# A graph layer with three places reordered: the fold of the query weights, the slice loop's divide, and the attention's inverse

## The reference

```
xn = layernorm(x)
x  = x + gnn(xn, edges) + mix(xn)
     gnn: filt = silu(attr @ Wf1 + bf1) @ Wf2 + bf2;  msg = xn[col] * filt
          agg = segment_sum(msg, row);  h = silu(agg @ Wu1 + bu1) @ Wu2 + bu2;  xn + batchnorm(h)
     mix: k = softmax(k, over nodes);  context = k^T v (8 heads of 32);  (q context) * gate @ Wproj + bproj
y  = layernorm(x)
     fx = y @ W_fx + b_fx;  w = softmax((y @ W_x + b_x) @ W_slice ..., over 64 slices, 8 heads)
     token = sum_n(fx * w) / (sum_n(w) + 1e-5)
     q, k, v = token @ W_q, token @ W_k, token @ W_v;  out = softmax(q k^T / 8) v
x  = x + (w out) @ W_out + b_out
```

## Time and profile before

| what | value |
|---|---|
| median of 3 runs | 2125.78 us (2119.08 to 2127.16) |
| profiled execution | 2126.19 us, span 2124.4 us |
| busy share PE / PEld / DVE / ACT / POOL | 89 / 72 / 71 / 63 / 68% |
| edge loop, first hidden product to last scatter | 151.2 to 1662 us |
| slice loop, first logits to last token product | 1820.2 to 2016.3 us |
| attention, to the first output product | 2016.6 to 2044.5 us |
| output products | 2044.5 to 2118 us |
| VectorE steps of the fold, L1350 / L1356 (two) / L1361 | 0.69 / 0.61 / 0.69 us |
| SP's queue in chunk 2: last window load before, next issue after | up to 191.8, from 197.05 us |
| VectorE steps L2158 / L2160 / L2165 / L2167 | 0.68 / 0.67 / 0.62 / 0.68 us |

### The profile page before, as it was taken

The page is one execution under the profiler, slowest core; times in us unless marked ns, Lnnn a source line. Parts: engine busy times, 40 slices in busy tenths (PEclk is TensorE's granted clock), DMA queues, the critical chain, the costliest instruction groups (busy, mean ns, idle before and its releaser), DMA issues. The chain is left out here.

```text
span 2124.4 us, 38305 instructions
## 1 busy us (share of the span) xinstructions
PE 1887.8 (89%) x9824; PEld 1537.4 (72%) x9824; DVE 1509.5 (71%) x3450; ACT 1347.4 (63%) x2410; POOL 1454.9 (68%) x997
## 2 busy tenths in 40 slices
PE   4988999899899989998899989998996397799998
PEld 3666888787777777777687767786775376577678
DVE  6966877777676767767677677676674297788746
ACT  4546766776676667666676676667664167577723
POOL 2216888888888888888888888888888574355500
PEclk9999999999999999999999999999998599899979
DMA  9777888987888789888888888888887892000002
GB/s 373 312 289 164 159 157 162 174 158 141 168 167 155 139 163 172 153 141 163 169 158 148 165 170 152 144 165 166 150 146 109 228 323 80 12 0 0 1 29 102
DMA packets 288979, 325.41 MB, mean 153 GB/s; under 512 B 30118, under 2 KB 251721, under 8 KB 288688
## 3 DMA queue, kind: packets, MB, share of 16 engines
q0 software_dynamic: 112896, 102.81, 39.2%
q1 hardware_dynamic: 172576, 217.21, 31.7%
q10 hardware_dynamic: 3280, 2.83, 0.5%
HBM read 167.64 MB, written 154.97 MB: 152 GB/s over the span
## 5 line engine op out<-in xcount | busy, mean ns | idle before, releaser
L993 POOL DMA_INDIRECT sums<-x_rows,out_idx x784 | 1238.1, 1579 | 291.4 <-issue 210.9
L1047 PE MATMUL bank<-wf,x_rows 128*128 128x256 f32 x3136 | 797.3, 382 | 0.0
L1047 PEld LDWEIGHTS bank<-wf,x_rows 128*128 128x128 f32 x3136 | 543.4, 191 | 53.5
L1157 ACT ACTIVATE x_rows<-bank,bf 128x512 f32<-128x512 f32 x392 | 270.3, 689 | 268.4 <-PE bank L1025 264.2
L1252 DVE TENSOR_TENSOR msg_low<-x_rows,msg_high 128x512 fp32r<-128x512 f32 x392 | 272.1, 694 | 170.8 <-ACT msg_high L1177 170.8
L1283 DVE TENSOR_TENSOR x_rows<-bank,x_rows 128x512 f32<-128x512 f32 x392 | 269.0, 686 | 105.1 <-PE bank L1047 99.8
L1177 ACT ACTIVATE msg_high<-x_rows 128x512 fp32r<-128x512 f32 x392 | 247.3, 631 | 93.0 <-DVE x_rows L1283 89.8
L1045 PE MATMUL bank<-gnn_bf_halves,ones 128*128 128x256 f32 x784 | 296.1, 378 | 0.0
L1165 ACT ACTIVATE x_rows<-pair 128x516 f32<-128x516 f32 x392 | 230.5, 588 | 78.5 <-DMA sums<-x_rows,out_idx 77.9
L1184 ACT ACTIVATE x_rows<-bank 128x512 f32<-128x512 f32 x392 | 231.9, 592 | 34.2 <-PE bank L1035 33.8
L1035 PE MATMUL bank<-window,spread 128*128 128x256 f32 x784 | 193.8, 329 | 60.9 <-DVE spread L1247 40.0
(11 more groups left out here) (330 smaller groups left out, 2729.4 us busy)
## 6 DMA issues: line engine op xcount, KB each, us to landing
window<-xn_halves SPq DMA_DIRECT2D x392, 128.0 KB, 4.1
sums<-gate SPq DMA_DIRECT2D x32, 800.0 KB, 10.4
x_rows<-id_rows SPq DMA_DIRECT2D x98, 256.0 KB, 5.2
x_rows<-attr_rows SPq DMA_DIRECT2D x98, 256.0 KB, 4.7
xn_halves<-xn_halves SPq DMA_DIRECT2D x7, 1792.0 KB, 6.6
x_rows<-id_rows SPq DMA_DIRECT2D x98, 128.0 KB, 3.7
sums<-x_rows,out_idx POOLq DMA_INDIRECT x784
res<-sums SPq DMA_DIRECT2D x24, 512.0 KB, 7.7
```

Source lines behind the costliest of these rows:

```text
L993: nc.gpsimd.indirect_dma_start(g.sums_dram[k], bass.IndirectOffsetOnAxis(ap=out_idx[:, ET * c + t:ET * c + t + 1], axis=0), summed[c % 2][ ...
L1047: mm = T.matmul(out, hidT[:, j // 2, f, ds((2 * (j % 2) + t) * P, P)], g.wf2[:, f, :], start=False, stop=f == CB - 1)
L1157: A.activation(hidT[:, h, f, :], hps[:], ACT.Silu, bias=g.bf1[:, f:f + 1]).then_inc(hid_ready, 1)
```

## The change

1. *Fold.* The three TensorE steps of the fold move to places 0, 2 and 4 of the loop's first group, and VectorE's answers to places 1, 3 and 5. Ahead of the loop TensorE only makes the hidden products and the first gather, now behind the first of them. The 13 weight loads move from place 2 to place 9.
2. *Slice loop.* VectorE divides tile t-1 before it shifts tile t. ScalarE's `round_both` is cut in two: `round_w(t-1)` ahead of the exponential, `round_x(t)` at the end of the step; copy of turned weights behind the exponential. POOL: `low_w(t-1)`, then `low_x(t)`. TensorE: turn_x(t+1) ahead of turn_w(t-2). The column sums of W_fx and W_q W_k^T are made in step 1, in the banks of the token sums, and read in step 2 before the token sums begin.
3. *Attention.* The sum of weights is taken as columns: eight products with the sums as stationary operand and one moving column give 128x4 numbers; VectorE scales and inverts these, writes two diagonal blocks, ScalarE two more, and four products of `mean_of` with the diagonals spread the inverse over 64 rows. The token is then (W_fx sums - eps bias) inverse + bias, in three wide VectorE steps. The bias products move to the block's start, and PSUM banks change names.

```diff
-AT_WEIGHTS = 2
+AT_WEIGHTS = 9
+AT_FOLD = (0, 2, 4)
...
+            def context():
+                pe.wait_ge(fold_stage, 1)
+                ...
+            def fold_query():
+                pe.wait_ge(fold_stage, 1 + CB)
...
             def output(s, place):
+                if is_first(s) and place == AT_FOLD[0]:
+                    turn_gram()
+                if is_first(s) and place == AT_FOLD[1]:
+                    context()
+                if is_first(s) and place == AT_FOLD[2]:
+                    fold_query()
...
             hidden(0, 0, 0, 0)
-            pe.wait_ge(fold_stage, 1)
...
+            gather(0, 0)
             hidden(0, 0, 0, 1)
-            pe.wait_ge(fold_stage, 1 + CB)
...
             hidden(0, 0, 1, 0)
-            gather(0, 0)
             along(pe, chunk, output)
...
             high_attr(0, 0)
-            for h, f in ((0, 0), (0, 1), (1, 0)):
-                silu(0, h, f)
+            silu(0, 0, 0)
             copy_rows(0, 0)
+            silu(0, 0, 1)
+            silu(0, 1, 0)
...
+            def weight_products():
+                pe.wait_ge(g.late_in, 16 * len(g.late_weights))
+                pe.wait_ge(small, ONES)
+                for h in range(FH):
+                    for b in range(CB):
+                        nc.tensor.matmul(acc[0][0:FD, ds(h, 1)], g.w_fx[:, b, ds(h * FD, FD)], g.mean_of[:, 0:1],
+                                         start=b == 0, stop=b == CB - 1)
+                nc.tensor.matmul(acc[1][0:FD, 0:FD], g.w_qT, g.w_kT, start=True, stop=True).then_inc(summed_w, 1)
...
             def step(t, r):
                 logits(t, r)
+                if exists(t + 1):
+                    turn_x(t + 1, (r + 1) % RING)
                 if not is_before(t, LAG):
                     turn_w(t - LAG, (r - LAG) % RING)
-                if exists(t + 1):
-                    turn_x(t + 1, (r + 1) % RING)
+                if is_known(t, 1):
+                    weight_products()
+                if is_known(t, LAG):
+                    pe.wait_ge(small, SHIFT_COPIED)
...
             def step(t, r):
+                if is_known(t, LAG):
+                    act.wait_ge(summed_w, 1)
+                    A.activation(g.mix, acc[1][0:FD, 0:FD], ACT.Copy).then_inc(small, 1)
+                if exists(t + 1):
+                    copy_xT(t + 1, (r + 1) % RING)
+                if not is_before(t, 1):
+                    round_w(t - 1, (r - 1) % RING)
+                expo(t, r)
                 if not is_before(t, LAG):
                     copy_w(t - LAG)
...
+                round_x(t, r)
...
             def step(t, r):
+                if is_known(t, LAG):
+                    weight_shift()
+                if not is_before(t, 1):
+                    divide(t - 1, (r - 1) % RING)
                 shift(t, r)
                 if exists(t + 1):
                     low_xT(t + 1, (r + 1) % RING)
-                if not is_before(t, 1):
-                    divide(t - 1, (r - 1) % RING)
...
+            dve.wait_ge(mat, COLS)
+            V.tensor_scalar(inv[:], g.ps[1][:, 0:HGB], EPS, 1.0 / C, ALU.add, ALU.mult).then_inc(vec, 1)
+            dve.wait_ge(vec, SCALED)
+            V.reciprocal(inv[:], inv[:]).then_inc(vec, 1)
+            dve.wait_ge(vec, INVERSE)
+            for q in range(2):
+                op = V.tensor_scalar(diag[:, ds(q * P, P)], g.ident[:], inv[:, q:q + 1], None, ALU.mult)
+            op.then_inc(vec, 1)
             dve.wait_ge(mat, FX)
-            dve.wait_ge(vec, SHARE)
-            V.tensor_tensor(raw, g.ps[3][0:FD, :], raw, ALU.add).then_inc(vec, 1)
+            V.tensor_tensor(heads(raw), heads(g.ps[3][0:FD, :]), wide(g.fx_less[:]), ALU.add).then_inc(vec, 1)
+            dve.wait_ge(mat, SPREAD)
             dve.wait_ge(vec, SUMMED)
-            V.tensor_tensor(fxT[:], raw, inv, ALU.mult).then_inc(vec, 1)
+            V.tensor_tensor(raw, g.ps[0][0:FD, :], raw, ALU.mult).then_inc(vec, 1)
+            dve.wait_ge(vec, DIVIDED)
+            V.tensor_tensor(heads(fxT[:]), heads(raw), wide(g.fx_bias[:]), ALU.add).then_inc(vec, 1)
...
+            for q in range(HGB):
+                for b in range(CB):
+                    mm = T.matmul(g.ps[1][:, ds(q, 1)], tokT[:, b, ds(q * P, P)], mean_of[:, 0:1], start=b == 0,
+                                  stop=b == CB - 1)
...
+            for q in range(HGB):
+                mm = T.matmul(g.ps[0][0:FD, ds(q * P, P)], mean_of[:], diag[:, ds(q * P, P)], start=True, stop=True)
```

More of the change, by code:

```diff
@@ L1303, in chunk, with turned_gram, scaled_context, folded_query @@
                     work(j)
-            def output(s, place):
+            def turned_gram():
+                dve.wait_ge(fold_made, 1)
+                V.tensor_copy(gram.rearrange("p b n -> p (b n)"), bankT[:]).then_inc(fold_stage, 1)
+            def scaled_context():
+                dve.wait_ge(cols_ready, 3)
+                dve.wait_ge(fold_made, 2)
+                for f in range(CB):
+                    V.scalar_tensor_tensor(out=ctx_m[:, f, :], in0=bankK[:, ds(f * P, P)], scalar=k_inv[:, f:f + 1],
+                                           in1=g.head_mask[:], op0=ALU.mult, op1=ALU.mult).then_inc(fold_stage, 1)
+            def folded_query():
+                dve.wait_ge(fold_made, 3)
+                V.tensor_copy(g.wqm[:], bankT[:].rearrange("p (b n) -> p b n", b=CB)).then_inc(fold_stage, 1)
+            def output(s, place):
+                if is_first(s) and place - 1 == AT_FOLD[0]:
+                    turned_gram()
+                if is_first(s) and place - 1 == AT_FOLD[1]:
+                    scaled_context()
+                if is_first(s) and place - 1 == AT_FOLD[2]:
+                    folded_query()
                 if place - 1 in AT_HIDDEN:
@@ L1863, in slice_tokens @@
     acc = token_sums(g)
+    summed_w, small = sem("h_summed_w"), sem("h_small")
+    ONES, SHIFT_COPIED = 1, 3
     heads = lambda ap: ap.rearrange("p (h n) -> p h n", h=FH)
@@ L2051, in step, with weight_shift @@
                     low_xT(t + 1, (r + 1) % RING)
-                if not is_before(t, 1):
-                    divide(t - 1, (r - 1) % RING)
+            def weight_shift():
+                dve.wait_ge(summed_w, 1)
+                V.scalar_tensor_tensor(out=g.fx_bias[:], in0=acc[0][0:FD, 0:FH], scalar=-float(C), in1=g.b_fxT[:],
+                                       op0=ALU.mult, op1=ALU.add).then_inc(small, 1)
+                dve.wait_ge(small, SHIFT_COPIED)
+                V.tensor_scalar(g.fx_less[:], g.fx_bias[:], -EPS, None, ALU.mult)
+            V.memset(g.mean_of[:], 1.0 / C).then_inc(small, 1)
             low_xT(0, 0)
@@ L2205, in _ @@
             A.activation(tokT[:, 0, :], acc[0], ACT.Copy).then_inc(act_done, 1)
-            act.wait_ge(mat, MIX)
-            A.activation(mix, g.ps[7][0:FD, 0:FD], ACT.Copy).then_inc(act_done, 1)
+            act.wait_ge(vec, INVERSE)
+            for q in range(2, HGB):
+                op = A.activation(diag[:, ds(q * P, P)], g.ident[:], ACT.Copy, scale=inv[:, q:q + 1])
+            op.then_inc(act_done, 1)
             high(0)
@@ L2245, in _ @@
             mm.then_inc(mat, 1)
+            pe.wait_ge(vec, DIAG)
+            pe.wait_ge(act_done, DIAG_COPIED)
+            for q in range(HGB):
+                mm = T.matmul(g.ps[0][0:FD, ds(q * P, P)], mean_of[:], diag[:, ds(q * P, P)], start=True, stop=True)
+            mm.then_inc(mat, 1)
             pe.wait_ge(vec, FX_DONE)
-            pe.wait_ge(act_done, MIXED)
-            T.matmul(g.ps[5][0:FD, :], mix, fxT[:], start=True, stop=True).then_inc(mat, 1)
+            T.matmul(g.ps[2][0:FD, :], g.mix, fxT[:], start=True, stop=True).then_inc(mat, 1)
             T.matmul(g.ps[1][0:FD, :], g.w_v, fxT[:], start=True, stop=True).then_inc(mat, 1)
@@ L2261, in _ @@
                 mm.then_inc(mat, 1)
[L2262 to L2264 removed]
             pe.wait_ge(vec, WEIGHED)
             for k in range(HALF_HEADS):
[L2267 removed]
+                mm = T.transpose(g.ps[5][0:FG, ds(k * P, P)], at[:, ds(k * FG, FG)], g.ident[:])
             mm.then_inc(mat, 1)
```

125 lines of the change are left out of this document (50 added, 75 removed).

## The result

The changed kernel takes 2103.36 us (median of 8 runs, 2094.23 to 2110.39); the kernel before takes 2123.34 us in the runs beside it (8 runs, 2118.78 to 2127.16). The ratio is 0.9903, 95% interval 0.9886 to 0.992: 0.97% less, 20 us. The prediction had 2110.5 us with a range of 2101 to 2119. The profiled execution of the changed kernel took 2107.18 us, its span is 2105.4.

What follows compares the result with a forecast made beforehand. The prediction took starved POOL at the edge loop's start, a three-engine circle of waits in the slice loop and the attention's chain as bounds; gains 5.0 + 6.3 + 4.2 = 15.5 from 2126.2 gave 2110.7, stated as 2110.5 us, range 2101 to 2119.

Steps and rivals of the forecast that it cites:

- rival (a): Attention: TensorE's clock stays up, gaining 9 to 10 us more, for 2101 us; chance 0.18.
- First scatter 2.4 us earlier: Edge loop's start: first filter product 3.8 us earlier, less 0.5 for transposes and 0.9 for half clock.
- What feeds POOL, 6.2 ahead less 1.2, gain 5.0: Edge loop's start: POOL's supply 6.2 us ahead by the 21st scatter, less 1.2 for TensorE's waits on VectorE.
- The ids' transfer: Edge loop's start: chunk 2's edge ids no longer behind weight loads; 4.4 us idle and 1.5 slow stretch saved.
- the fold's work in the loop: Edge loop's start: two big fold steps cost 2.1 us, waits for VectorE's added steps 1.2.
- Rival (b): Edge loop's start gains nothing, since loads at place 9 starve VectorE once, 4.6 us; 2115.7 us, chance 0.12.
- Slice loop, 3.66 a tile: Slice loop: tile falls from 3.83 to 3.66 us, limits being 3.53, 3.54 and 3.63; whole gain 6.3 us.
- The small products in step 1: Slice loop's step 1: 17 small products take up to 4 us at half clock, partly hidden; cost 1.6 us.
- (c): Slice loop: the tile stays at 3.75 to 3.83 us as another close limit takes over; 2117 us, chance 0.12.
- (d): Slice loop: ScalarE's exponential is late, 4.36 us a tile, 24.5 us lost; 2141 us, chance 0.06.
- Last tile, 0.5: Slice loop's end: the divide of tile 47 is out of the way before the last shift, gaining 0.5 us.
- Attention, 3.2 to `fxT` and 1.0 for the bias products: Attention: `fxT` complete 3.2 us earlier, bias products leaving their place gain 1.0; together 4.2 us.

Runs made afterwards that it cites:

- e5: The changed kernel itself, run again with a second profile; 2098.91 us, ratio 0.9881 to the kernel before.
- e11: The kernel before with only the weights' loads moved to place 9; 2117.8 us, ratio 0.9965.
- e7: The changed kernel with token-sum products 64 columns wide and two unused 512-column products where TensorE waits; 2098.21 us, ratio 0.9892 to the kernel before.
- e2: The kernel before with the slice loop's new orders on all four engines, without the early sums; 2117.04 us, ratio 0.9965.
- e4: The kernel before with VectorE's new order alone (divide of tile t-1 before shift of tile t); 2116.49 us, ratio 0.9965.
- e12: The kernel before with the fold's move, the loads' place and VectorE's order, nothing else; 2113.36 us, ratio 0.9944.
- e1: The kernel before with the edge loop's part alone (fold moved, weight loads at place 9); 2114.23 us, ratio 0.9962.

## Why the prediction was right, and which steps were not

The total lay within the range, and the places were right, but the gain came out at 20 us where the sum had 15.5. By stretches, and with the mean of the changed kernel's three profiles, the largest part of the difference is 3.4 us from the last logits to the end (109.6, where the sum had 113.0), mainly the full clock of e5; the slice loop has 1.2 more than the sum, the start 0.9. The median lies below the forecast's own 2105 to 2115 us, and the whole range holds it because rival (a) had widened it down to 2101. By its own steps, with the means of the like profiles:

- **First scatter 2.4 us earlier**: 2.5 on the mean, but 1.8 against profiles with as long a half clock as the one that I computed from, and 3.0 with a longer one. The fold's two large products were 1.05 us each at full clock, as said.
- **What feeds POOL, 6.2 ahead less 1.2, gain 5.0**: 5.9. But its terms were off in both directions. The ids' transfer was put at 5.9 (4.4 idle and 1.5 of slow stretch) and is worth 4.6; the fold's work in the loop was put at 3.3 (2.1 + 1.2) and costs 1.2. The prediction named the transfer as the largest piece and then spoke of the fold; e11 says that one constant would have done three quarters of it. (Between the ids' turn and their issue stood eleven loads, all that the program issues at that place, not the 13 that I wrote; their 6.6 us on SP, 165.81 to 172.45, are right.) Rival (b), loads at place 9 starving VectorE, did not happen.
- **Slice loop, 3.66 a tile**: 3.63, my bound of the circle, without the reserve I had added for TensorE's own 3.53 and the transposes' 3.54. Limits that close to each other cost nothing here: 45 x 0.03 is 1.4 us. The small products in step 1 took 2.32 us at a clock that rose midway in the first profile; in e7 they ran at half clock for 3.57:

```profile
1820.99 3.57 PE L1971 MATMUL pair<-mean_of,wide_weights 128*64 128x1 f32 x32
1824.49 0.47 PE L1973 MATMUL pair<-wide_weights 64*64 64x64 f32 x2
```

  Over the kernels with and without them, tiles 0 to 3 take 14.9 and 13.6 us on the mean: 1.3, of my 1.6, though the kernels of either group lie further apart than that (12.4 to 14.5 and 12.8 to 17.4). Rivals (c) and (d) did not happen (the 24.5 us of (d) should read 24.3); the exponential starts 0.03 us after the shift's end (1991.46 + 0.70 to 1992.19).
- **Last tile, 0.5**: 0.5 to 0.6, from the last logits to the attention's first product (10.15 to 9.56, 9.63 with VectorE's order alone). The whole stretch hides it: with the new loop order and the old attention it takes 118.1 on the mean of three, with both old 117.4, so what follows the last tile lost 1.3.
- **Attention, 3.2 to `fxT` and 1.0 for the bias products**: here a step failed as I put it. At the full clock the way to `fxT` is as laid out: 6.98 us from the bias products to the product from `fxT` in e5, 10.01 from the first product to the same place before, so 3.0. What failed is the silent assumption that this stretch keeps its full clock as it did before. It does in some runs (e5) and not in others (0.2 gained in the first profile), and where it does not, TensorE happens to have the full clock back for Q, V and the logits, which gave 2.4 behind `fxT`; the output products gave 1.6, where the half clock lasted 4.4 us into them and not 6.7. The term came out at 4.2 with other contents. The one-column products were put at 1.5, at most 1.7, and took 1.92 at full clock (e5).
- **Rival (a), 9 to 10 us more if the clock stays up**: 8.0 more (104.6 and 112.6), in two of five profiles. I gave it 0.18 as something that either is or is not; it should have been a share of the runs, and the range's lower end should have been lower than 2101: nine of 18 runs lie below it, the lowest at 2093.9. Its argument, less idle time, fits only in part. All six profiles with 3.0 to 4.0 us of idle ahead of `fxT` had fallen before W_out and both with 0.44 had not, but the idle time of 1.49 us is the same in e5, which stayed up, and in the first profile, which did not. What I had set against the rival, that narrow products never brought the clock up again, does not hold: in the first profile it came back at 2010.9, behind the products with W_fx and the spread. The Trainium skill, "TensorE: Matmul & The Clock Gate", section "What's actually happening", says of the other change, the first rise of the clock at a kernel's start, that it is "run-variable" for one and the same kernel. Here the falls are so too: the first one stands 11.6, 26.8 and 13.1 us behind the last logits in three profiles of this kernel.

## What to carry to other kernels

When an engine's queue holds something needed at once behind something needed much later, move that first, and alone: eleven loads at another place brought 4.6 us, the rebuilt fold 1.3. When an engine order is changed in a circle of waits, try each engine by itself: one engine's order brought 7.4 of 8.6 us, and the wait that looked like the cause stayed and cost next to nothing. Cost a chain of narrow products at both clocks, and say in how many runs each may hold; a product into an unused bank, where TensorE waits anyway, is cheap to try (it cost nothing in one place and 0.8 us in another), but judge it by many runs.

## What the runs showed that I had not expected

- The granted clock of one and the same kernel falls in different places from run to run, and the whole kernel's time moves by 8 us with it, in the profiles and in the 18 runs by their granted clock.
- A product with 1 moving column and one with 64 take the same time here: 16 in 1.92 and in 1.97 us, at full clock, 128x128 stationary.
- What runs ahead of a stretch seems to bear on its clock: with VectorE's new order and the old attention the clock fell first 13.0, 12.1 and 10.8 us behind the logits of tile 48 (e2, e4, e12), with both old 20.5 to 21.1 us behind them (before, e1, e11). From the attention's first product to the end the first three took 1.3 us more on the mean. Three profiles of each are few, and why it is so is not shown.
- From the 21st scatter to the last the nine profiles with the fold moved spread over 7 us (1448.7 to 1455.8), the five without over 1.5 (1450.6 to 1452.0), e11 among them, whose start is not starved either. A part is a longer mean scatter; the rest, and whether the difference is more than chance, is open.
